# A new interleaving for eight batches: order of the turns, PSUM banks and zero products

## The chip, the cores and the metric

The kernel runs on one core of one Trainium2 chip. The metric is device time in microseconds (us), from three timed runs of the program. PE is the matmul engine and PEld its weight load; DVE, ACT and POOL are the vector, scalar and GpSimd engines; SP issues most of the DMAs. PSUM has eight banks, which only PE writes and only DVE and ACT read.

## What is computed

Four transformer layers over x of 8 batches x 256 rows x 128 features, fp32. Each layer is a gated cross attention to a context of the same shape (16 heads of 8 features) and a gated feed-forward block:

```python
x = x + tanh(g_xattn[l]) * cross_attention_l(layernorm(x), ctx)
x = x + tanh(g_ffn[l])   * ffn_l(layernorm(x))
```

Layer 2's attention is causal; layer 3's keeps only the 51 queries with the highest mean cosine score in each head. The feed-forward blocks are: layer 0 a GELU on the 192 rows with the highest router scores; layer 1 a mixture of 8 gated experts (top 2) and a shared one; layer 2 a mixture of 8 experts of width 512 (top 2, exact GELU) and a shared one; layer 3 one product whose input and weight are rounded to a 6-bit grid.

## The kernel before

Every batch is a stream of the same 286 steps, written out by `stream_steps`: `stats` and `norm` (layer norm), `turn` (transposing the rows), `keys` and `query` (projections), eight `maxima` steps a layer (six in layer 2; a tile of scores on PE, L865, whose row maxima DVE takes, L1389), `max_turn`, eight `attend` steps (scores turned, L888, whose exponential ACT takes, L757) with eight `weigh` steps (probabilities times values, L906), `heads`, `heads_turn`, `project`, and the layer's feed-forward steps: `route0`, `hidden` and `output` (L1046 and L1056 in layer 1, L1077 and L1086 in layer 2), `quantise` and `affine3` in layer 3. Four batches are in flight at once; batch b+4 takes over the buffers of batch b.

One list, `SCHEDULE`, holds the 8 x 286 = 2288 steps in one order, and every engine walks that one list and does its own part of each step. `TURNS_TAKEN` is that order: a string of 2288 digits, each naming the batch whose next step comes. So each engine's instructions stand in the order of the list, and an engine that waits for one step holds all its later ones.

```python
left = [iter([(step, b, l, part) for step, l, part in stream_steps()]) for b in range(BATCHES)]
return [next(left[int(b)]) for line in TURNS_TAKEN.split() for b in line]
```

`BANKS_TAKEN` holds 1857 digits, one for each product that takes a PSUM bank, in the order of the list. Ahead of a product PE waits (`wait_bank`) until the bank's last holder has been read by DVE or ACT. `SCRATCH` names steps ahead of which PE makes a number of products of zeros into the bank that it takes next (L838, 512 columns of bf16): they compute nothing that is used.

PE's products come in four tile forms, by the rows and columns of the array that they use: 128x128 (projections, transposes, feed-forward, zero products), 64x128 (`maxima`, `attend` and the causal masks: two row tiles side by side), 128x32 (`weigh`: four column tiles; `max_turn` and small transposes) and a few with 9 or 16 rows (32x128: `chosen`, `out_bias`). An fp32 product is two passes with a weight load each; a `hidden` step is two pairs of products, into two banks, one after the other.

After a `query` product ACT writes its bf16 high part and the fp32 copy, POOL splits the rest into two more parts (L600, L603, L605), and SP moves the parts with six DMAs (L508) to the rows that the scores read; the first `maxima` of the layer waits for all six.

Of the kernel before, what the change touches and what calls it, by code (L numbers as in the profile page):

```python
# [128 lines left out]


TURNS_TAKEN = """
0002012001311331020003100000202003000101213111001100110011001101200210202020120120023101212121122322
1311102110031333100310120012022101010200300023121022212333232321301012211212131121323313231203031023
3012002320333302023302232220323212300130210303001021010210310101030013033033013301300201333101121210
1212131232212102020000100102121023222102232232212233021211212033320232203210011123020110111010200100
2301322211122011101212121212221122303013303103310321221303030322033232230221332330311202101331103013
0103332200221002012023213310121302102310121222011330221201203032112020210130013311002231322001320100
2012000001001031001313211000110002101010011110211200203011120101112220320103002001111211212123001231
1120220100112001032122101211211221112123302023020012120332002223202003222120300200231111122022120312
0220220012330100031020002001330033010000013013103300002213223230311231103112311332303102231121131123  # L140
1130132112122111111310333101323133101233302233013022002320303000003021303311230130033121124131344411
3111311343142333132232221321555534242353344354443424434322443442342233252223455232234542554544554455
4254544525223453334343455424333545544254242453535535345324434554455354342424552433433452353355323345
3323353322335423325353265366535533635345645644453544344345363466534634434666446466444666663454346453
4334563644366333664366356635336646446564566464565345666356367747546744565656554664674446746546664654
4445757567567557757775747574777547444665455775557676776475774676455775755576554545777655555756575576
7775546555466655445766657464544667667676467776767767456476646564455665446674665666546674665447666666
6566666576766556445747557676744574775547545545574446675756576776747676476475644445477766554547544447
5446664745454575547656775475744475766465774745657767747667454444777766577777566747546577466665547477
4656545766555457544655564474475454455465457577465467774575567667557646755554755674574474576457576766  # L150
6666474665447656747456774644676476756665777776656577557466666664547774644557544765554647567557656764
6774465467557477776777776777777547775545667766765775774645666776764767767457444466764576774455554454
4665477676556566656654656565665564666464665777777567656756676657757776746766547556645776777776657477
4577577767767675775776574777677657475765474564757775647646777647546477767777745757654677
"""


# [9 lines left out]
def signals(step, b, l, part):  # L167
# [44 lines left out]


BANKS_TAKEN = """
1023546012345671002345671023456701253406712503456703124056341203567401236740123406123456701234560123
4501623457620456712405673051246730145261302630245763017634560731425607312674031240673451267034501267
5674520167324501367242501450671245067123045670126745016372450167321452367145671230674501267450124567
0412375604231045623014567230156732017562301474562301627435016235704165234701634572016573240615732641
0567312475612345673401273512640736124012735640123456710237456702340256734256340756120734056741207456
0712560713256071325647132564135264103526401725640175642017536427016534207165430271564302756143027561  # L220
4307265143072561430725614037256147032561470325614730256340172534670125234670123546012345760123456707
1234567013245067132450673124531674531456731456731045367145326745236745672304516702345672304567023407
5614714723470235603417520634175206531725306217503621753061725361072365014762301542367015236740123670
1436701253456701253467015634750167345201762357016572340156723420143560123456017234572013472506134721
5064725106472310645725632304567234567230145671230145674523601734562134721567234015670156347012345671
2045671204536712456312734056712043567012347506123470152347051234017256340172456720145672013452367045
6712031456270134562301425346012576340124576012745601327645013624570126730451236750123067152301675023
4162357014623567401234607120734607123047651247613204762103642701634270162734126734612734126753412567
3041256340125634250172345701234567102375601237560162013756123467512364751326475312653470132650471265
0471265042376145072361045723160457216035472160354726103456712034561234705671203465127034126572301243  # L230
5340712503476123450762304576230764502376145023761452307614507231654072350164523016452301654230165423
0165402316540312653401734560341756340563401756345017634017643107346521076345210745210745712045126045
360124501623456012637450312674503167450324516032745160324
"""

SCRATCH = {
    ("turn", 1, 0, 0): 11, ("keys", 3, 0, 0): 1, ("maxima", 0, 0, 7): 1, ("maxima", 1, 0, 0): 7,
    ("max_turn", 0, 0, 0): 6, ("attend", 0, 0, 0): 1, ("turn", 1, 4, 0): 1, ("turn", 0, 1, 0): 4,  # L240
    ("heads", 2, 0, 0): 1, ("heads", 3, 0, 0): 1, ("heads_turn", 3, 0, 0): 2, ("heads", 0, 1, 0): 1,
    ("heads_turn", 0, 1, 0): 3, ("attend", 1, 1, 0): 4, ("attend", 2, 1, 0): 8, ("heads_turn", 5, 0, 0): 3,
    ("turn", 4, 1, 0): 1, ("turn", 5, 4, 0): 3, ("maxima", 4, 1, 0): 6, ("maxima", 4, 1, 1): 1,
    ("turn", 5, 1, 0): 6, ("maxima", 6, 0, 3): 1, ("heads", 5, 3, 0): 2, ("maxima", 7, 3, 5): 4,
    ("heads_turn", 5, 3, 0): 5, ("heads_turn", 6, 3, 0): 1, ("heads_turn", 7, 3, 0): 5, ("turn", 4, 7, 0): 31}
VALUES_SCRATCH = 7


# [1352 lines left out]
```

How the kernel before makes its waits and increments, by code:

```python
        @block.sync  # L519
# [13 lines left out]
                sp.dma_start(dst, src).then_inc(values_loaded, 16)  # L533
            for s in range(1, SLOTS):
                load_x(s, s)
                load_ctx(s, s)
            w = Walk()
            for w.i, (step, b, l, part) in enumerate(SCHEDULE):
                s = b % SLOTS
                if step == "load_x" and b + SLOTS < BATCHES:
                    sp.wait_ge(sems["xb_ready"], w.at_step("xb_ready", 1, "max_parts", b, 0, 0))
                    load_x(b + SLOTS, s)
                if step == "load_ctx" and b + SLOTS < BATCHES:
                    sp.wait_ge(sems["a_full"], w.at_step("a_full", 1, "keys", b, LAYERS - 1, 0))
                    load_ctx(b + SLOTS, s)
                if step == "load_weight3" and b == 0:
                    sp.wait_ge(sems["a_full"], w.at_step("a_full", 1, "key_mean", b, SPARSE, 0))
                    sp.dma_start(w3_sb, w3).then_inc(w3_loaded, 16)
                if step in ("keys", "query"):
                    name, terms, st, parts = (("k", K_TERMS, k_st[s], k_parts[s]) if step == "keys"
                                              else ("q", Q_TERMS, q_st[s], q_parts[s]))
                    if b < SLOTS and l == 0:
                        sp.wait_ge(*CLEARED[s])
                    if step == "keys" or b >= SPLIT_STREAMS or l > 0:
                        sp.wait_ge(sems[f"hi_ready{s}"], w.at(f"hi_ready{s}", 1))
                        move_parts(sp, terms, 0, st, parts, sems[f"{name}_moved{s}"])
```

## Time and profile before

| | |
|---|---|
| median of 3 runs | 955.25 us (954.61 to 955.75) |
| profiled execution, first to last instruction | 952.3 us |
| the profiled execution's own time | the page gives its span alone; the median lies 2.95 us over it |
| PE busy | 890.7 us |
| DVE busy | 711.9 us |
| ACT busy | 639.7 us |
| POOL busy | 497.8 us |

A piece in the chain of waits or the timeline is a start, a length and what ran. Matmuls are pipelined, so a piece of the timeline ends later than the next one can start; start to start is what a piece costs. In the rows by stretch PEclk is TensorE's granted clock as a share of full speed.

### The profile page before, as it was taken

To read this page: it belongs to the slowest core of one execution; us is meant where nothing else is said; L and a number is where in the kernel's file an instruction comes from. 1 tells how busy PE (TensorE), PEld (TensorE's weight loads), DVE (VectorE), ACT (ScalarE), POOL (GpSimd) and SP (SyncE) were. 2 spreads that over 40 slices of the span, in tenths; PEclk is the share of its full clock that TensorE was granted. 3 is DMA by queue.
4 is the path that set the end of the run, shared out by engine and by line. 5 is a ranking of instruction groups with operands and counts; after the bars stand their busy time and mean duration, and the time that the engine had idled before them with its cause. 6 is when DMAs were issued, how large, how long until landed. Compare 5 with 4: busy or idle time off the path is not lost.

```text
span 952.3 us, 22705 instructions
## 1 busy us (share of the span) xinstructions
PE 890.7 (94%) x8025; PEld 609.1 (64%) x8025; DVE 711.9 (75%) x2175; ACT 639.7 (67%) x1460; POOL 497.8 (52%) x627
## 2 busy tenths in 40 slices
PE   7898889998999999899987999999999999999976
PEld 3344446864799987468643366746588987878533
DVE  6997988868553268986998999887745346666897
ACT  2785766676784635788776677777797448687851
POOL 5446554776872135655356365657772525533172
PEclk9998999999999999999999999999999999999999
DMA  5433341321010010001102121111110010000000
GB/s 149 118 96 83 77 111 30 90 64 37 16 35 23 2 46 7 21 25 51 47 21 68 26 60 34 36 36 36 26 47 2 15 38 1 20 19 18 20 3 24
DMA packets 67520, 39.95 MB, mean 42 GB/s; under 512 B 8263, under 2 KB 65376, under 8 KB 67408
## 3 DMA queue, kind: packets, MB, share of 16 engines
q1 hardware_dynamic: 62608, 30.44, 12.5%
q0 software_dynamic: 2208, 6.78, 2.6%
q8 instruction: 67, 1.10, 0.5%
q10 hardware_dynamic: 2592, 1.26, 0.5%
q14 instruction: 45, 0.37, 0.1%
HBM read 11.12 MB, written 1.05 MB: 13 GB/s over the span
## 4 chain that ended last, share of the span: by engine, by line
PE 63%; DVE 17%; POOL 6%; issue 6%; ACT 5%; DMA 1%; SPq 1%; DVEq 0%; POOLq 0%; ACTq 0%
PE banks L1086 12%; PE banks L1077 12%; PE banks L906 7%; DVE mx L1389 7%; PE banks L1046 6%; PE banks L888 4%; PE banks L865 4%; PE banks L1056 3%; PE banks L851 3%; ACT probs L757 3%; POOL h L617 3%; PE banks L1015 2%; PE banks L844 2%; POOL rn L664 2%; PE banks L955 1%
## 5 line engine op out<-in xcount | busy, mean ns | idle before, releaser
L1389 DVE TENSOR_REDUCE mx<-banks 128x4 f32<-128x1024 f32 (+1 forms) x240 | 283.9, 1216 | 25.0 <-PE banks L865 18.0
L757 ACT ACTIVATE probs<-banks 128x512 f32<-128x512 f32 (+1 forms) x512 | 258.8, 582 | 57.1 <-PE banks L888 53.9
L810 ACT ACTIVATE probs<-banks,b_sb 128x256 f32<-128x256 f32 x288 | 117.9, 474 | 72.9 <-PE banks L1077 71.5
L906 PE MATMUL banks<-probs,v_aug 128*9 128x256 f32 (+1 forms) x2048 | 147.7, 370 | 7.4 <-ACT probs L757 6.2
L1086 PE MATMUL banks<-w_sb,probs 128*128 128x128 f32 x1152 | 140.6, 277 | 0.2 <-ACT probs L757 0.2
L1086 PEld LDWEIGHTS banks<-w_sb,probs 128*128 128x128 f32 x1152 | 134.9, 192 | 5.7 <-issue 2.5
L1077 PE MATMUL banks<-hT,w_sb 128*128 128x256 f32 x576 | 137.4, 382 | 0.1
L610 POOL TENSOR_TENSOR rstd<-veps,mhalf 128x2 f32<-128x2 f32 x64 | 46.3, 724 | 165.3 <-DVE veps L1336 164.7
L664 POOL TENSOR_TENSOR rn<-ss,mhalf 128x32 f32<-128x32 f32 x16 | 88.0, 5501 | 53.2 <-DVE ss L1184 53.1
L1077 PEld LDWEIGHTS banks<-hT,w_sb 128*128 128x128 f32 x576 | 104.4, 190 | 14.8 <-DVE xs L1260 0.8
L1260 DVE SCALAR_TENSOR_TENSOR xs<-banks,comb,xs 128x128 f32<-128x128 f32 x144 | 43.7, 344 | 83.2 <-PE banks L1086 83.0
L888 PE MATMUL banks<-q_st,k_st 64*128 64x256 bf16 (+1 forms) x1024 | 93.9, 269 | 8.9 <-issue 5.7
L865 PE MATMUL banks<-k_st,q_st 64*128 64x256 bf16 (+1 forms) x1024 | 89.0, 265 | 10.4 <-DVE mx L1389 5.1
L617 POOL TENSOR_SCALAR h<-xs,mv,rstd 128x128 f32<-128x128 f32 x112 | 90.9, 818 | 5.9
L888 PEld LDWEIGHTS banks<-q_st,k_st 64*128 64x128 bf16 x1024 | 35.3, 94 | 73.2 <-issue 30.5
L642 POOL TENSOR_TENSOR xs<-xs,raw 128x256 f32<-128x256 f32 x72 | 52.9, 735 | 53.3 <-ACT raw L798 50.8
L1046 PE MATMUL banks<-hT,fc_sb 128*128 128x256 f32 x320 | 77.0, 384 | 0.0
L688 ACT ACTIVATE hT<-banks 128x256 f32<-128x256 f32 x96 | 36.9, 389 | 59.4 <-PE banks L844 59.0
L906 PEld LDWEIGHTS banks<-probs,v_aug 128*9 128x9 f32 x2048 | 34.4, 88 | 62.1 <-ACT probs L757 25.8
L865 PEld LDWEIGHTS banks<-k_st,q_st 64*128 64x128 bf16 x1024 | 37.7, 94 | 56.7 <-issue 18.6
L648 POOL TENSOR_SCALAR_AFFINE_SELECT probs<-probs 128x512 f32<-128x512 f32 x64 | 40.6, 644 | 54.1 <-ACT probs L757 54.0
L1046 PEld LDWEIGHTS banks<-hT,fc_sb 128*128 128x128 f32 x320 | 57.8, 190 | 8.2 <-issue 0.6
(198 smaller groups left out, 1484.0 us busy)
## 6 DMA issues: line engine op xcount, KB each, us to landing
k_st<-k_parts SPq DMA_DIRECT2D x192, 64.0 KB, 2.1
q_st<-q_parts SPq DMA_DIRECT2D x186, 64.0 KB, 2.1
w_sb<-in_w POOLq DMA_DIRECT2D x16, 256.0 KB, 3.7
fc_sb<-in_fc POOLq DMA_DIRECT2D x6, 256.0 KB, 4.3
x_in<-in_x SPq DMA_DIRECT2D x8, 128.0 KB, 4.1
cT<-in_ctxT SPq DMA_DIRECT2D x8, 128.0 KB, 3.1
out_x<-xs SPq DMA_DIRECT2D x8, 128.0 KB, 1.8
q_st<-mT SPq DMA_DIRECT2D x32, 16.0 KB
```

Source lines behind the costliest of these rows:

```text
L617: ins = nc.gpsimd.tensor_scalar(h[s][:, r, :], (x_in if l == 0 else xs)[s][:, r, :], mv[s][:, r, 0:1], rstd[s][:, r:r + 1], ALU.subtract, ...
L642: nc.gpsimd.tensor_tensor(xs[s][:, :, :].rearrange("p t d -> p (t d)"), xs[s][:, :, :].rearrange("p t d -> p (t d)"), raw[s][:, n % OUT_RI ...
L664: nc.gpsimd.tensor_tensor(rn[s][:, :], ss[s][:, :], mhalf[:, :], ALU.pow)\
L757: nc.scalar.activation(probs[s][:, part % UNIT_RING, 2 * a:2 * a + 2, 0:n], b_bank(w, a + 1)[:, 0:2 * n].rearrange("p (j q) -> p j q", j=2 ...
L810: ins = nc.scalar.activation(hid[s][:, part % UNIT_RING, c, :], b_bank(w, half + 1)[:, j * ROWS:(j + 1) * ROWS], ACT.Gelu, bias=b1_sb[:, p ...
L865: ins = nc.tensor.matmul(a_bank(w, a + 1)[:, i * keys:(i + 1) * keys], head_rows(q_st, s, a, hp0 + i, r * P, P), head_rows(k_st, s, a, hp0 ...
L888: ins = nc.tensor.matmul(b_bank(w, a + 1)[:, j * n:(j + 1) * n], head_rows(k_st, s, a, 2 * g + j, t * P, P), head_rows(q_st, s, a, 2 * g + ...
L906: ins = nc.tensor.matmul(c_bank(b, l, u // 4)[VW * i:VW * i + VR, g % 2, q0:ROWS], v_aug[s][:, t, 4 * g + i, :], probs[s][:, u % UNIT_RING ...
L1046: ins = nc.tensor.matmul(a_bank(w, k + 1)[:, a * ROWS:(a + 1) * ROWS], fc1_sb[:, 2 * part + k, a, :], hT[s][:, :], start=True, stop=True)
L1077: ins = nc.tensor.matmul(b_bank(w, half + 1)[:, j * ROWS:(j + 1) * ROWS], w1_sb[:, part, 2 * half + j, :], hT[s][:, :], start=True, stop=True)
L1086: ins = nc.tensor.matmul(a_bank(w, 1)[:, r * D:(r + 1) * D], hid[s][:, part % UNIT_RING, c, r * P:(r + 1) * P], w2_sb[:, part, c, :], star ...
L1389: nc.vector.tensor_reduce(mx[s][:, r, :, hp0:hp0 + n], banks[:, first:first + 2, :].rearrange("p a (n k) -> p a n k", n=n), AX.X, ALU.max) ...
```

## The change

Three tables get new contents, and no instruction of the steps themselves changes: the order (`TURNS_TAKEN`), the banks (`BANKS_TAKEN`), and the places and numbers of the zero products (`SCRATCH`; 28 places with 121 products become 25 with 125). The 2288 steps and 1857 banks stay as many. The new order was searched with a count of PE's changes of tile form among its costs. The two long tables are cut here to their first lines; the third is whole.

```diff
 TURNS_TAKEN = """
-0002012001311331020003100000202003000101213111001100110011001101200210202020120120023101212121122322
+0002102331001320011010220002000000101011033111310110110020012001201200212003020220122103201112122303
...
 BANKS_TAKEN = """
-1023546012345671002345671023456701253406712503456703124056341203567401236740123406123456701234560123
+1022123450612634507123471256341256341721561207534601256734061270346712013452671534126734501267305126
...
 SCRATCH = {
-    ("turn", 1, 0, 0): 11, ("keys", 3, 0, 0): 1, ("maxima", 0, 0, 7): 1, ("maxima", 1, 0, 0): 7,
-    ("max_turn", 0, 0, 0): 6, ("attend", 0, 0, 0): 1, ("turn", 1, 4, 0): 1, ("turn", 0, 1, 0): 4,
-    ("heads", 2, 0, 0): 1, ("heads", 3, 0, 0): 1, ("heads_turn", 3, 0, 0): 2, ("heads", 0, 1, 0): 1,
-    ("heads_turn", 0, 1, 0): 3, ("attend", 1, 1, 0): 4, ("attend", 2, 1, 0): 8, ("heads_turn", 5, 0, 0): 3,
-    ("turn", 4, 1, 0): 1, ("turn", 5, 4, 0): 3, ("maxima", 4, 1, 0): 6, ("maxima", 4, 1, 1): 1,
-    ("turn", 5, 1, 0): 6, ("maxima", 6, 0, 3): 1, ("heads", 5, 3, 0): 2, ("maxima", 7, 3, 5): 4,
-    ("heads_turn", 5, 3, 0): 5, ("heads_turn", 6, 3, 0): 1, ("heads_turn", 7, 3, 0): 5, ("turn", 4, 7, 0): 31}
+    ("maxima", 0, 0, 0): 27, ("query", 2, 0, 0): 4, ("maxima", 1, 0, 0): 2, ("maxima", 1, 0, 1): 2,
+    ("maxima", 1, 0, 2): 1, ("maxima", 1, 0, 3): 5, ("max_turn", 0, 0, 0): 2, ("attend", 0, 0, 0): 1,
+    ("attend", 0, 1, 0): 8, ("attend", 1, 1, 0): 4, ("turn", 3, 1, 0): 2, ("attend", 1, 3, 0): 2,
+    ("turn", 3, 3, 0): 2, ("heads_turn", 4, 0, 0): 2, ("attend", 3, 3, 0): 5, ("maxima", 4, 1, 4): 1,
+    ("maxima", 4, 1, 7): 1, ("attend", 4, 1, 0): 8, ("heads_turn", 3, 3, 0): 3, ("heads_turn", 5, 1, 0): 3,
+    ("maxima", 7, 3, 0): 2, ("maxima", 7, 3, 2): 3, ("maxima", 7, 3, 5): 1, ("heads_turn", 7, 3, 0): 3,
+    ("turn", 4, 7, 0): 31}
```

A key of `SCRATCH` is (step, batch, layer, part).

## Rows read from the trace of the kernel before

**Rows 1.** The page: span, and each engine's busy time, share and instructions.
```profile
span 952.3 us, 22705 instructions
PE 890.7 (94%) x8025; PEld 609.1 (64%) x8025; DVE 711.9 (75%) x2175; ACT 639.7 (67%) x1460; POOL 497.8 (52%) x627
```

**Rows 2.** By stretch: length; busy PE, PEld, DVE, ACT, POOL; PEclk, DMA share, GB/s.
```profile
470.00:600.00 130.00, 117.16 (x1162) 61.75 (x1159) 122.92 (x349) 91.73 (x209) 73.10 (x99) 1.00 0.17 44
...
700.00:900.00 200.00, 199.34 (x1645) 162.66 (x1643) 116.00 (x407) 143.45 (x310) 81.23 (x85) 1.00 0.08 19
...
886.00:952.30 66.30, 52.55 (x489) 26.30 (x487) 56.45 (x229) 31.55 (x67) 28.14 (x32) 0.99 0.06 17
```

**Rows 3.** The chain that ended last, 350 to 358 us: start, length, what.
```profile
350.43 1.79 PE banks L1086 x16
...
352.65 1.73 PE banks L1077 x8
354.37 0.33 PE banks L865 x4
...
354.92 0.22 PE banks L865 x4
...
355.57 1.98 PE banks L1086 x16
```

**Rows 4.** Groups by line and shape: count, busy us, mean ns, idle before and releasers.
```profile
L1389 DVE TENSOR_REDUCE mx<-banks 128x4 f32<-128x1024 f32 x224 | 265.3, 1216 | 21.8 <-PE banks L865 18.0 <-PE banks L873 3.3
L757 ACT ACTIVATE probs<-banks 128x512 f32<-128x512 f32 x448 | 239.3, 608 | 51.4 <-PE banks L888 48.2
...
L906 PE MATMUL banks<-probs,v_aug 128*9 128x256 f32 x1792 | 136.5, 384 | 7.2 <-ACT probs L757 6.2
...
L838 PE MATMUL banks<-zeros 128*128 128x512 bf16 x128 | 34.0, 393 | 5.3 <-DVE mx L1389 3.7 <-ACT resid L724 1.6
...
L844 PE MATMUL banks<-ident,h 128*128 128x128 f32 x128 | 26.2, 289 | 9.3 <-POOL h L617 4.9 <-POOL h L659 2.5 <-DVE h L1345 1.5
```

**Rows 5.** Timelines of PE, ACT, POOL, SP round one query (batch 7, layer 0).
```profile
568.70 0.70 PE L955 MATMUL banks<-hT,wqk 128*128 128x256 f32 x2
...
576.44 0.39 PE L865 MATMUL banks<-k_st,q_st 64*128 64x256 bf16 x4
...
571.58 0.67 POOL L605 TENSOR_TENSOR q_parts<-resid,q_parts 128x256 bf16<-128x256 f32 x1
...
569.93 3.78 SPq L508 DMA_DIRECT2D q_st<-q_parts  x6
```

**Rows 6.** Who waited for whom on PE: us in total, times, longest us.
```profile
PEld banks L906 <- ACT probs L757: 25.8, 72, 1.2
...
PEld banks L865 <- DVE mx L1389: 15.9, 33, 1.0
PEld banks L844 <- DVE resid L1417: 11.8, 16, 1.5
```

**Rows 7.** Short stretches round the low clocks, columns as in rows 2.
```profile
19.10:22.60 3.50, 3.27 (x9) 2.30 (x9) 3.50 (x6) 0.84 (x2) 0.95 (x2) 0.51 0.64 172
...
77.20:80.60 3.40, 1.09 (x8) 0.85 (x8) 1.80 (x6) 0.55 (x2) 2.52 (x5) 1.00 0.86 189
80.60:84.00 3.40, 2.69 (x14) 1.51 (x14) 0.90 (x3) 2.34 (x5) 0.00 (x0) 0.50 0.61 160
84.00:87.40 3.40, 3.40 (x30) 0.83 (x29) 1.62 (x11) 1.09 (x3) 2.01 (x3) 0.50 0.00 0
...
142.00:145.40 3.40, 3.40 (x24) 2.01 (x20) 0.54 (x2) 2.06 (x4) 0.00 (x0) 0.50 0.00 0
```

More of the change, by code:

```diff
@@ L131 @@
 TURNS_TAKEN = """
-0002012001311331020003100000202003000101213111001100110011001101200210202020120120023101212121122322
[L133 to L151, printed above, removed]
@@ L152 @@
-6774465467557477776777776777777547775545667766765775774645666776764767767457444466764576774455554454
-4665477676556566656654656565665564666464665777777567656756676657757776746766547556645776777776657477
-4577577767767675775776574777677657475765474564757775647646777647546477767777745757654677
+0002102331001320011010220002000000101011033111310110110020012001201200212003020220122103201112122303
+2110000303323133110323033301101220120012003212010201231312002211011112133113123112330113122130330222
+1120033300230320230122032210210323200321203100023120010121300013323102330330113301013113320302231010
@@ new lines @@
+1212112012112201233211300123201220103102211022032230122303112200102223300021110210022201201201001120
+0112102111332121222202012121222311233110303322221222100322022303332303010312121033110310030310321230
+0200233121203001201232301013101022101311200232101230333211202023131003031031022022130300211203301123
+1000103000210113001201000100222011220113131101120323000231211301012022230020001200020011211101010030
+1221323122123320311310123111023122221111132310120132310002212122000022202121220022000202330131213112
@@ new lines @@
+1102103021022132321332300101332100100130000320013200033110313001110110101332121100132110301012010321
+2313313021331032302033311131330120302102303020122001231003300323013131013223002414222412423121421221
+2231313412312131313121231123222525433445353442245334442533442434323224433425235253455325442454422545
+4554534543343544345244353433425454544533354552323433543455544544442344425322332233453255322345323333
+4523325323663353365635344644546444534354546565345635654335664543434543564346545646636364346633543463
@@ new lines @@
+3445433364336636466633464566556656656643655645565436663453467677765444454646457654764646646654644454
+5656775477465476757755775447577575477456547675577567447654776675776567776655675757455475565765667766
+7466646564647664755664655565655676465656565757445576654647764666666657774747576667664645754755665545
+5464577466754754755675754675675574567564544455477654745775675774475445777575756467767464754454754566
+4455745756477644544746457547474664454675477776576674774555775775547666757777646564667777666447674474
@@ L155 @@
+4476455655665677746656444564777546667665465747445644756676665564666654777657555657647746657476477475
+7757454655667675676477765766767556675766766656756677567777544467646677767776764574777757555557775674
+7677775555777775657766455667665774767574476757475747646554454456545574475556455465544556455455446575
+7564447545775756656474466456567646767454677676667766476646566576665646476774576674767764757756774755
+4774767475776757774764776547754776756456577667767466465677766774756744777776565456746777
 """
@@ L214 @@
 BANKS_TAKEN = """
-1023546012345671002345671023456701253406712503456703124056341203567401236740123406123456701234560123
[L216 to L233, printed above, removed]
+1022123450612634507123471256341256341721561207534601256734061270346712013452671534126734501267305126
+7045120621456710124503674531426174514356010610761537167617716504157145623456701423556623457623674521
@@ new lines @@
+6014526016721450321064523076067457023167045042546442650120510645764501673456701326452701764520167423
+4501623745203726014263240132564723560124501261261345234564246352461265165243156341207512072514201742
+5601523456206234534601234012763407561561341561340712563470120516345301364573012643567420135426405120
+1152034521735401723541573645635470134203274204723147247317431740563710473470307414710171704130301410
+3043041043034030343010347073014567304634567013676363701301313107364512303540351267435671245614165126
@@ new lines @@
+7412535312675673512456731734562506345062074526012642301430173043407123476237157612353560153674530671
+2304267230467231045067612706410120647026140216026170625372537543267401523017532013475013475201534003
+4512674512067124503160723602367456723014532672323456015635643501267051245610210425640520420513135134
+5165010165021623014672301467230164440612670312346701340125616734156561273405630633673063706456745674
+3126704512346712346721346726234717346247105467065415475047140570123457012364501752306741234516720670
@@ new lines @@
+1672346502346735401345670154672014563740134101562340142305267203427013475632013425343475013501403151
+3407147107532603527025626702675417452012734567230145267364014573670163456701726452301645162346572532
+5236451045607123071704170412310236723015675236014527360137601321362163612074536347051236015320132506
+7234673642051676157570167076010160617235601723707012563470120717071017304217042304237015251023571614
+6237164523610623107071201210272070720702707270107270125634713713456702030562301456723245252340156730
@@ L234 @@
+5634715673415671020362074514071264507321452312374523172451037245603745620560247156204125056120701562
+370175014752301301425402175235725372542334544453543721441
 """
 SCRATCH = {
-    ("turn", 1, 0, 0): 11, ("keys", 3, 0, 0): 1, ("maxima", 0, 0, 7): 1, ("maxima", 1, 0, 0): 7,
-    ("max_turn", 0, 0, 0): 6, ("attend", 0, 0, 0): 1, ("turn", 1, 4, 0): 1, ("turn", 0, 1, 0): 4,
-    ("heads", 2, 0, 0): 1, ("heads", 3, 0, 0): 1, ("heads_turn", 3, 0, 0): 2, ("heads", 0, 1, 0): 1,
-    ("heads_turn", 0, 1, 0): 3, ("attend", 1, 1, 0): 4, ("attend", 2, 1, 0): 8, ("heads_turn", 5, 0, 0): 3,
```

## The prediction

> **What bounds the kernel now.** I read the page first: PE is busy for 94% of the span, DVE for 75% [rows 1]. Then the busy times by stretch, which say where that average holds. From 700 to 900 us PE is busy for 199.3 of 200 us, and DVE for 116; from 470 to 600 us DVE has 122.9 of 130 us and PE 117.2; in the last 66 us DVE has 56.5 and PE 52.6 [rows 2]. So PE sets the time in the feed-forward stretches, and DVE in the middle, where batches 0 to 3 hand over to 4 to 7 and the row maxima crowd (1.216 us each [rows 4]), and at the end. Last the chain of waits, for what one product costs on PE.
>
> A busy PE is not yet a PE at its own pace, so I summed the least start-to-start times. Eight passes of L1077 take 1.73 us and sixteen of L1086 1.79 us where the product before has the same tile form [rows 3]. With the like for every kind, and with each change of form at its price below, all 8025 passes come to 841 us of the 952.3. What lies over that is waits and start, some 104 us, and the largest releasers are the exponentials, the maxima and DVE's other results [rows 6].
>
> **The change, part by part.** No step is added or dropped. I walked both orders through the kernel's own step list and counted.
>
> **Changes of tile form.** A four-pass tile of scores takes 0.22 us behind scores and 0.33 us behind another form, so a change costs 0.11 us. L1086 takes 1.98 us behind one against 1.79 us, 0.19 us, since the second pass's weights aren't hidden either [rows 3]. The old order makes 768 changes, the new one 791, though the search counted them. Into scores 26 more (287 to 313), into two-pass fp32 products 3 more, into `weigh` and small transposes 6 fewer: 26 x 0.11 + 3 x 0.19 - 6 x 0.11 = +2.8 us. The page "TensorE: Matmul & The Clock Gate" of the Trainium skill, section Single matmul latency, puts some 166 ns over the streaming on a product that can't hide its drain; by that an estimate of +3.8 us would stand for these 23 changes. The row decides, and the sum goes on with 2.8.
>
> **Zero products.** 125 in place of 121 at 0.216 us, the time of one pass of 256 fp32 columns (1.73 / 8 [rows 3]), which is also their start to start: +0.9 us. Bounds: nothing, where they fill a wait (their group shows waits for DVE ahead [rows 4]), and +2 us at the low clock. Together PE's own pace grows by 3.7 us.
>
> **Waits for results.** For each step of PE I took PE's own work between it and the step whose result it needs, set it against the least time that the old trace shows for such a hand-over, and counted what is lacking, each wait once (a distance is longer by the waits already counted inside it). For the old order this gives 62 us, stretch by stretch in the places where the trace has its 104. The rest is start-up, low clock and engines that come late, and I take it as equal. For the new order it gives 72 us, in four kinds:
> - A `weigh` behind its exponentials (two of 0.608 us [rows 4]): 9.2 us becomes 4.7.
> - Other hand-overs (`heads` to `heads_turn`, layer norm to `turn`, `max_turn` to `attend`): 27.5 becomes 16.5. `turn` waits on POOL and DVE now [rows 4, 6].
> - The first scores behind their `query`. The last part leaves POOL at 572.25, SP issues six moves for 3.78 us, and the scores start at 576.44, 7.0 us after the query's product ended and 7.4 after its last pass began [rows 5]. The old order leaves PE less than these 7.4 us of its own work in 13 of 32 cases, the new one in 18, often 5.3 to 5.9 us: 10.2 becomes 19.5 us.
> - Banks that PE wants back before they are read. In the old order a quarter of all takings come within 1.83 us of the last holder's product, in the new one within 1.50; short ones rise from 119 to 250. A bank of `turn` or `heads_turn` needs 0.75 us, one of a pair of exponentials 1.5, one of maxima 1.8: 15.4 becomes 31.2 us.
>
> That is -4.5 - 11.0 + 9.3 + 15.8 = +9.6 us. Two stretches I don't take from this count, because DVE binds there. In steps 1050 to 1390 the count says +5.7 us, but DVE's work exceeds PE's by 19.9 us in the old order and 20.2 in the new, so +0.3. From the last layer-2 product on (886 us) DVE's steps sum to 67.8 us by the rows' durations in the old order, 81.0 in the new (eleven maxima and 54 `choose` parts stand behind it, against 8 and 37). The trace makes 56.45 us of the 67.8 [rows 2], so the new ones make 67.4. The stretch had 66.3 us, 9.85 more than DVE's busy time; with the same lag it takes 77.3. PE's own part grows from 46.5 to 53.3 us, which the total holds already, so 11.0 - 6.8 = +4.2 us, against -1.0 in the count. Waits are then 9.6 - 5.4 + 5.2 = +9.4 us. The least times of chains that the old order never presses are too long, by 0.1 to 0.2 us in some 15 places (`heads`, `keys`, `route0`): -2 us. So +7.4.
>
> **The clock.** PEclk is 0.51 in 19.1 to 22.6 us and 0.50 in 80.6 to 87.4 and 142.0 to 145.4, each behind a stretch in which PE did little (1.09 of 3.4 us in 77.2 to 80.6) [rows 7]. The 27 zero products ahead of the first scores (5.8 us) fill the wait before the first fall; but DVE is busy for 3.50 of 3.50 us there, so its going gives nothing. The other two, at most half of 10.2 us, 5 us, may go, or others of that size may come. I take 0.
>
> ACT's table loads, the DMAs and POOL's work stay off the path: ACT and POOL have a quarter of the span free or more [rows 1], and rows 2 show neither at its limit. If that cover went, it would show as longer hand-overs, which are in the bounds.
>
> **Sum.** 3.7 + 7.4 = +11.1 us on a profiled execution of 952.3 us, 963.4; the median lies 2.95 us over that span, so 966.
>
> **The rivals.**
> - *Banks cost nothing (faster).* The mechanism is the choice of banks in the new order: where a bank is taken straight back, the product that takes it waits for a later result anyway, or the reader has come in time. Then the 15.8 us go, and 966.4 - 15.8 = 951 us. For it: the hand-overs to `weigh` and `turn` do get longer distances, and many short takings are of a `query` behind its own `turn`, where PE waits in any case. Against it: the count takes each wait once, and most of the short takings are scores or `hidden` products with no other wait. It decides if PE's waits for banks stay below some 5 us over the old ones.
> - *Pressed banks and late readers (much slower).* With less slack, readers that come late now reach PE. With the fifth percentile of the old trace's hand-over times instead of the least, the count is 75.6 and 97.3 us, +21.7; with 3.7 that is 981 us.
> - *The transfers are hidden.* The waits ahead of a layer's first scores fall into the same time as others, on DVE's side, and the 9.3 us don't show: 957 us, at the edge of no change.
> - *The change doesn't do what it says*: the count of form changes rises rather than falls; that is in the sum.
>
> **How the numbers follow.** The main forecast has 0.45, banks that cost nothing 0.25, hidden transfers 0.14, pressed banks 0.16. A measurement of this kernel tells some 0.2% (1.9 us) from no change. Slower by more is 0.45 + 0.16 + 0.08 of the hidden transfers, 0.69; the other 0.06 of them is no change; faster is 0.25. The likeliest case alone spans 958 to 975 (the clock's 5 us, the zero products' 2 and the correction of 2 either way). Over the cases the range is 948 to 982: below lies the faster rival with a better clock, above the slowest with a worse one.
>
> **What would show it.** In the new profile: the sum of PE, DVE and ACT work as before; L865's idle time ahead of it grown by about 10 us through the DMAs of `q_st`; waits of `hidden` and scores for ACT and DVE readers grown; waits of L906 for L757 and of L844 for its inputs smaller; the stretch behind the last L1086 about 77 us long, with DVE busy for 67; more tiles of L865 and L888 at 0.33 us. I am wrong if PE's waits for banks don't grow, or if the end takes 66 us or less.

## The result and the profile after

The changed kernel takes 969.1 us in the median of four runs (965.41 to 970.47), the kernel before 954.93 (950.34 to 955.75) beside it: ratio 1.0156, 95% interval 1.0134 to 1.0179 (the two medians alone give 1.0148), slower. The forecast was 966 us, in a range of 948 to 982. The profiled execution took 968.79 us with a span of 967.0, 14.7 us more than the span in [rows 1].

The page of the kernel after, its span and busy times:

```profile
span 967.0 us, 22712 instructions
...
PE 898.4 (93%) x8029; PEld 607.3 (63%) x8029; DVE 715.3 (74%) x2175; ACT 639.6 (66%) x1458; POOL 497.9 (51%) x627
```

The work of DVE, ACT and POOL is that of [rows 1] to within 3.4 us, so the 14.7 us are PE's own pace and PE's waits. Four groups by line and shape of the kernel after, columns as in [rows 4]:

```profile
L906 PE MATMUL banks<-probs,v_aug 128*9 128x256 f32 x1792 | 136.3, 382 | 4.9 <-ACT probs L757 3.5 <-ACT raw L764 0.3 <-ACT resid L724 0.3
...
L865 PE MATMUL banks<-k_st,q_st 64*128 64x256 bf16 x896 | 83.6, 276 | 10.8 <-DMA q_st<-q_parts 3.8 <-DVE mx L1389 3.1 <-ACT probs L757 1.9
...
L838 PE MATMUL banks<-zeros 128*128 128x512 bf16 x132 | 37.0, 417 | 17.2 <-DVE mx L1389 5.7 <-DVE resid L1417 3.9 <-DVE junk L1450 2.2
...
L844 PE MATMUL banks<-ident,h 128*128 128x128 f32 x128 | 25.4, 284 | 4.0 <-POOL h L617 2.4 <-POOL h L659 1.0 <-ACT probs L757 0.2
```

The waits that were to shrink did: ahead of `weigh` (L906) 7.2 us became 4.9, ahead of the layer norm's `turn` (L844) 9.3 became 4.0. The zero products (L838) are the surprise: 5.3 us of waiting ahead of them [rows 4] became 17.2. They compute nothing and need no result; all that they can wait for is the bank that they write. PE's waits on others in the kernel after, as in [rows 6], show the same three movements and a wait for the queries' moves that has grown:

```profile
PEld banks L906 <- ACT probs L757: 18.3, 56, 1.0
...
PEld banks L865 <- DVE mx L1389: 13.0, 32, 1.0
PEld banks L865 <- DMA q_st<-q_parts: 10.0, 12, 2.1
...
PEld banks L844 <- DVE resid L1417: 7.7, 11, 1.7
PEld banks L838 <- DVE resid L1417: 5.0, 4, 1.5
```

The wait for the queries' moves in the kernel before:

```profile
PEld banks L865 <- DMA q_st<-q_parts: 1.3, 2, 0.6
```

To put a kind to each wait I took every start-to-start of PE that exceeds, by over 0.05 us, the least that its pair of kinds needs in the old trace, and gave it to the reader or result whose end came last before it. The last column is an experiment, told below.

| waits of PE, us | before | after | change forecast | change measured | new_timed_banks |
|---|---|---|---|---|---|
| banks | 29.7 | 45.2 | +15.8 | +15.5 | 29.7 |
| first scores behind `query` | 0.8 | 5.0 | +9.3 | +4.2 | 8.2 |
| `weigh` behind exponentials | 11.0 | 7.4 | -4.5 | -3.6 | 7.6 |
| other hand-overs | 36.0 | 26.3 | -11.0 | -9.7 | 31.0 |
| not placed | 10.0 | 9.6 | | -0.4 | 11.2 |
| sum | 87.5 | 93.5 | +9.6 | +6.0 | 87.7 |

With what is under 0.05 us each and with the slow clock, all that lies over PE's own pace is 103.8 us before and 111.5 after, +7.7. By the same pairs of kinds the own pace is 841.3 and 847.5 us, +6.2.

The sizes in this table depend on how the products are grouped, the signs don't. A coarser grouping of the same traces (each product by its kind, and by whether the one before it and the one behind it have its tile form) gives an own pace of 836.6 and 840.6 us, +4.0; waits for banks of 30.8 and 55.3 us, and 32.4 in new_timed_banks; and first scores behind their `query` of 1.7, 8.8 and 9.0 us.

Where it lies along the order, in us, from the first product of a step to that of another:

| kernel | to step 300 | 300 to 1050 | 1050 to 1390 | 1390 to end |
|---|---|---|---|---|
| before | 127.0 | 331.6 | 110.7 | 383.0 |
| after | 133.8 | 324.7 | 121.7 | 386.8 |
| new_timed_banks | 128.2 | 322.7 | 119.0 | 384.8 |
| new_then_old | 135.9 | 324.4 | 121.0 | 382.8 |
| old_then_new | 127.9 | 329.1 | 125.0 | 385.0 |
| old_few | 132.0 | 335.0 | 112.6 | 388.6 |
| old_timed_banks | 125.2 | 328.8 | 113.1 | 385.7 |

### The profile page after: what moved, and what is told of

The parts are those of the page before. It is cut to its first block, busy times and chain, and to the rows that moved or that the text cites. A ratio compares the mean times of both kernels' runs of the same rounds, so it can differ in the third digit from the quotient of the medians.

```text
span 967.0 us, 22712 instructions
## 1 busy us (share of the span) xinstructions
PE 898.4 (93%) x8029; PEld 607.3 (63%) x8029; DVE 715.3 (74%) x2175; ACT 639.6 (66%) x1458; POOL 497.9 (51%) x627
## 4 chain that ended last, share of the span: by engine, by line
PE 68%; DVE 15%; ACT 5%; issue 5%; POOL 3%; DMA 2%; SPq 1%; DVEq 0%; POOLq 0%; ACTq 0%
PE banks L1077 13%; PE banks L1086 13%; PE banks L906 7%; PE banks L1046 5%; PE banks L865 5%; PE banks L888 5%; DVE mx L1389 4%; PE banks L851 4%; ACT probs L757 3%; PE banks L1056 3%; PE banks L838 2%; PE banks L1015 2%; PE banks L844 2%; DMA q_st<-q_parts 1%; PE banks L920 1%
## 5 line engine op out<-in xcount | busy, mean ns | idle before, releaser
L1389 DVE TENSOR_REDUCE mx<-banks 128x4 f32<-128x1024 f32 (+1 forms) x240 | 283.9, 1215 | 33.7 <-PE banks L865 26.3
L906 PE MATMUL banks<-probs,v_aug 128*9 128x256 f32 (+1 forms) x2048 | 147.4, 369 | 4.9 <-ACT probs L757 3.5
L1086 PE MATMUL banks<-w_sb,probs 128*128 128x128 f32 x1152 | 141.3, 277 | 0.1
L1077 PE MATMUL banks<-hT,w_sb 128*128 128x256 f32 x576 | 138.9, 386 | 0.1
L1086 PEld LDWEIGHTS banks<-w_sb,probs 128*128 128x128 f32 x1152 | 135.0, 192 | 5.8 <-issue 2.8
L1077 PEld LDWEIGHTS banks<-hT,w_sb 128*128 128x128 f32 x576 | 103.2, 190 | 17.3 <-DVE xs L1260 3.3
L1260 DVE SCALAR_TENSOR_TENSOR xs<-banks,comb,xs 128x128 f32<-128x128 f32 x144 | 43.6, 344 | 79.8 <-PE banks L1086 77.3
L865 PE MATMUL banks<-k_st,q_st 64*128 64x256 bf16 (+1 forms) x1024 | 89.9, 268 | 11.9 <-DMA q_st<-q_parts 4.8
L865 PEld LDWEIGHTS banks<-k_st,q_st 64*128 64x128 bf16 x1024 | 37.4, 95 | 57.7 <-issue 17.6
L906 PEld LDWEIGHTS banks<-probs,v_aug 128*9 128x9 f32 x2048 | 34.7, 88 | 58.4 <-issue 23.5
```

Of the source, the lines that this page charges most:

```text
L865: ins = nc.tensor.matmul(a_bank(w, a + 1)[:, i * keys:(i + 1) * keys], head_rows(q_st, s, a, hp0 + i, r * P, P), head_rows(k_st, s, a, hp0 ...
L906: ins = nc.tensor.matmul(c_bank(b, l, u // 4)[VW * i:VW * i + VR, g % 2, q0:ROWS], v_aug[s][:, t, 4 * g + i, :], probs[s][:, u % UNIT_RING ...
L1077: ins = nc.tensor.matmul(b_bank(w, half + 1)[:, j * ROWS:(j + 1) * ROWS], w1_sb[:, part, 2 * half + j, :], hT[s][:, :], start=True, stop=True)
L1086: ins = nc.tensor.matmul(a_bank(w, 1)[:, r * D:(r + 1) * D], hid[s][:, part % UNIT_RING, c, r * P:(r + 1) * P], w2_sb[:, part, c, :], star ...
L1389: nc.vector.tensor_reduce(mx[s][:, r, :, hp0:hp0 + n], banks[:, first:first + 2, :].rearrange("p a (n k) -> p a n k", n=n), AX.X, ALU.max) ...
```

## The experiments

A median is that of the runs of its group, and each ratio is to the kernel before on the same chip.

**Halves of the change.** Four kernels take a part of the change each. new_other_banks and old_other_banks replace the table of banks in the new and in the old order by one that a plain rule gives (the bank whose reader has been done longest, by the sums of the prediction):

```diff
 BANKS_TAKEN = """
-1022123450612634507123471256341256341721561207534601256734061270346712013452671534126734501267305126
+0123456721034567012345671234560123457601234571023645671023450162340156273457016534675034526701523460
...
```

> The new order and the new zero products, with the 1857 banks given anew: each product takes the bank whose last reader was done longest ago (a pair of neighbours for scores and heads), improved a little by single changes. Theory: banks taken back too early cost the new kernel about 15 us more than the old one; by PE's own distances the counted waits for banks fall from 31.3 to 14.2 us, and all waits, each counted once, from 71.9 to 64.7. So about 7 us faster than the new kernel: 962 us, with fewer stalls on readers of L1389 and L757. Rival (banks cost nothing, the products wait for a later result anyway): 969 us, within 2.

Measured: 971.31 us, ratio 1.0178 (1.0156 to 1.02).

> The old order and old zero products, with banks given by the same rule of the longest done reader. It is the control for the rule. The count for the old order is 15.5 us of waits for banks with its own banks and 21.4 with these, all waits 62.3 and 67.4. Theory (banks count): about 5 us slower than the old kernel, 960 us. Rival (banks cost nothing): 955, within 2.

Measured: 974.24 us, ratio 1.0218 (1.0198 to 1.0237). The same rule costs the old order 20 us and the new one 2, so the first of the two, read alone, would have said that banks don't matter. With its control it says only that the rule is bad: it has no rows of when a reader really ends, and the waits put to banks rise from 29.7 to 50.8 us in the old order. What the control does show is that the table of banks by itself can be worth 2%.

new_old_zeros is the kernel after with the zero products of the kernel before:

```diff
 SCRATCH = {
-    ("maxima", 0, 0, 0): 27, ("query", 2, 0, 0): 4, ("maxima", 1, 0, 0): 2, ("maxima", 1, 0, 1): 2,
...
+    ("turn", 1, 0, 0): 11, ("keys", 3, 0, 0): 1, ("maxima", 0, 0, 7): 1, ("maxima", 1, 0, 0): 7,
...
```

> The new order and banks, with the old kernel's table of zero products (the same steps, 121 products). This tells the table of zero products from the order. PE's own pace falls by 2.5 us (779 changes of form in place of 791, four products fewer); the waits that the new table fills come back: 81.0 us counted in place of 71.9. Theory (the order and its banks carry the loss): 969 to 976 us, since zero products mostly stand in waits. Rival (the zero products and the 20 or so changes of form that they bring carry the loss): 960 us or less.

Measured: 972.72 us, ratio 1.0201 (1.0177 to 1.0225). The loss isn't in where the zero products were put: with the old places it is as large or a little larger.

new_then_old has the new order, banks and zero products to step 1050 and the old ones behind, for the steps that are left (three banks had to be changed at the seam):

```diff
 TURNS_TAKEN = """
...
-2231313412312131313121231123222525433445353442245334442533442434323224433425235253455325442454422545
+2231313412312131313121231123222525433445353442245335434443434434434233252223455232234542554544554455
...
```

> The new order, its banks and zero products up to step 1050, then all that is left in the old order with the old banks and zero products (three banks changed at the seam). In both traces step 1050 begins 458.5 us from the start, so what the new order loses in steps 0 to 300 it has won back by there. Theory: the loss of the new kernel lies behind step 1050, so this one takes the old kernel's time and what the seam costs: 955 to 960 us. Rival (a part in the first 1050 steps hands its loss on to what follows, through batches that stand less far): 965 to 970 us.

Measured: 962.32 us, ratio 1.0093 (1.0069 to 1.0116), between the two. Its row in the table by stretch says more than its time: 1050 to 1390 takes 121.0 us though the old order stands there, and what follows takes the old time.

**Banks by the trace.** new_timed_banks keeps the new order and the new zero products, and chooses each bank by the ends of the readers in the trace of the kernel after; old_timed_banks does so for the old order from its own trace.

```diff
 BANKS_TAKEN = """
-1022123450612634507123471256341256341721561207534601256734061270346712013452671534126734501267305126
+0112125673401234567012304567012345012675341207645301275634051260345621072314675123456712034567012345
...
```

> New order and zero products, but each product takes its bank by the changed kernel's own trace: the one whose reader ended with most to spare (searched over the whole list, pairs kept side by side). In that trace 84 takings start less than 0.12 us behind the reader of their bank, 26.6 us in all; with these banks, at the same times, 24 do, 7.4 us. Theory (the new table of banks carries the loss): the difference of 19 us goes, and the time falls to 950 to 956 us. Rival (behind each wait for a bank PE would have waited for a result anyway, or the engines that read have no time to spare): not under 963 us. Second rival (the stretch from step 1050 to 1390, where DVE sets the pace, doesn't move with the banks, all else does): 958 to 962.

Measured: 956.3 us, 12 runs, ratio 1.0034 (1.0011 to 1.0056). Of the 15 us that the change costs (ratio 1.0156) some 12 go with this one table. The first theory holds, at the upper end of what it gave and far from the rival's 963 us. The second rival's premise holds too, but for little: from step 1050 to 1390 the time moved only from 121.7 to 119.0 us, while the first 300 steps got back 5.6 us (133.8 to 128.2).

> Control: old order and zero products, banks chosen in the same way from the old kernel's trace. There 26 takings start less than 0.12 us behind their reader, 7.4 us, and with these banks 21 would, 5.0 us. Both theories: 950 to 956 us, no difference or a small gain. If the way of choosing is itself at fault, as the rule of the second run was (+20 us on the old order), it shows here, and the run before says nothing against the banks.

Measured: 955.04 us, 12 runs, ratio 1.0013 (0.9997 to 1.0029): no difference. So the old table was already as good as this way of choosing makes one, and the new table wasn't.

The gain isn't the clock's alone, though the clock has a part in it. (The mean granted clock is that of a whole run, as a share of full speed.) The runs of new_timed_banks differ by 9 us, the slowest with the lowest mean granted clock (962.38 us at 0.983, 953.33 at 0.996). At the same clock of 0.996 a run of the kernel after took 965.41 us, so 12 us lie between the two tables there too, run for run.

One number of those two expectations was poor. Of the 1857 takings 80 have a last holder whose reader I hadn't matched; I had set its end 1.5 us behind the product, and most of the 26.6 us came from them. Without them, the takings within 0.3 us of their reader's end are 253 before, 438 after, 171 in new_timed_banks and 228 in old_timed_banks. They tell the same.

One place shows how a bank costs time. PE's timeline of the kernel after:

```profile
102.67 0.39 PE L865 MATMUL banks<-k_st,q_st 64*128 64x256 bf16 x4
105.24 2.45 PE L838 MATMUL banks<-zeros 128*128 128x512 bf16 x8 [2.18 <-DVE junk L1450]
107.62 0.61 PE L888 MATMUL banks<-q_st,k_st 64*128 64x256 bf16 x4
```

And DVE's, with the last reading of the router's bank, then the same steps on PE in new_timed_banks:

```profile
104.70 0.47 DVE L1450 SCALAR_TENSOR_TENSOR junk<-banks,col,before 128x256 f32<-128x256 f32 x1
```

```profile
99.31 0.39 PE L865 MATMUL banks<-k_st,q_st 64*128 64x256 bf16 x4
99.79 1.90 PE L838 MATMUL banks<-zeros 128*128 128x512 bf16 x8
102.26 0.40 PE L888 MATMUL banks<-q_st,k_st 64*128 64x256 bf16 x4 [0.57 <-DVE junk L1450]
```

SP's move of the row maxima, which this `attend` needs, in the kernel after and in new_timed_banks:

```profile
103.23 0.58 SPq L569 DMA_DIRECT2D q_st<-mT  x1
```

```profile
100.28 0.58 SPq L569 DMA_DIRECT2D q_st<-mT  x1
```

Eight zero products stand ahead of an `attend` to fill its wait for that move. (The last row names L1450 in its place; but in new_timed_banks L1450 had ended at 101.66, and the scores start 1.98 us behind the start of the move.) In the kernel after the bank of the zero products is the router's, which DVE reads until 105.17, some 1.94 us behind the start of the move; so they start only when the wait that they should fill is over, and the scores come 4.95 us behind the tile before (102.67 to 107.62). With another bank they run inside the wait, and it is 2.95 us. Over the whole kernel the waiting ahead of L838 falls back from 17.2 us to 5.0, with the same 132 products in the same places (125 of `SCRATCH` and seven that both kernels have at the start). Group of new_timed_banks:

```profile
L838 PE MATMUL banks<-zeros 128*128 128x512 bf16 x132 | 34.6, 395 | 5.0 <-DVE mx L1389 3.4 <-ACT probs L757 1.1 <-ACT resid L724 0.4
```

The first group, the 27 ahead of the first scores, in the kernel after and in new_timed_banks:

```profile
11.55 7.33 PE L838 MATMUL banks<-zeros 128*128 128x512 bf16 x27 [1.41 <-DVE v_aug L1309]
```

```profile
11.13 5.99 PE L838 MATMUL banks<-zeros 128*128 128x512 bf16 x27
```

In the first the products wait for a bank, and the granted clock is 0.50 from 10.9 to 14.3 us. In the second they don't wait, and the clock is 1.00 over the first 514 us. This suggests that a wait for a bank costs clock too; no run sets the clock apart.

old_then_new is the other half, old to step 1050 and new behind:

```diff
 TURNS_TAKEN = """
...
-3111311343142333132232221321555534242353344354443424434322443442342233252223455232234542554544554455
+3111311343142333132232221321555534242353344354443422222423442434323224433425235253455325442454422545
...
```

> The other half: the old order, banks and zero products up to step 1050, then the new order's for the steps that are left. The changed kernel lost 10.9 us from step 1050 to 1390 and 3.8 us behind. With the new order up to 1050 and the old one behind it, the stretch 1050 to 1390 still took 121.0 us, against 110.7 in the old kernel, and what follows took the old time. Theory (what the order up to 1050 leaves over for the stretch of the maxima sets its length): it now takes some 111 us, and the whole 956 to 959 us. Rival (the new arrangement behind 1050 costs by itself): the stretch takes 118 us or more, and the whole 964 to 969 us.

Measured: 970.46 us, ratio 1.017 (1.0142 to 1.0197): the rival's side and past its range, with 125.0 us from 1050 to 1390. As the new order up to 1050 with the old one behind it had also lost there, neither half carries the loss alone: each mixture of the two orders is longer there than the old one, with banks that weren't chosen for it. By the coarser grouping their waits for banks are 45.5 us (new_then_old) and 50.4 (old_then_new) against 30.8 in the kernel before, so the banks are the likelier cause; no run gives these two orders, unchanged, banks by their own traces.

**Fewer changes of form.** new_few takes new_timed_banks and moves 43 steps by one to five places, each where PE's own pace and the counted waits together came out lower; old_few does it with 26 steps of the old order, hyb_few with 40 of new_then_old. The banks are chosen again from the traces. The first moves of old_few:

```diff
 TURNS_TAKEN = """
-0002012001311331020003100000202003000101213111001100110011001101200210202020120120023101212121122322
+0002012001311331020003100000202003000110213111001100110011001101202010202020120120023101212121122322
...
```

> The changed order with 43 steps moved by one to five places so that PE changes its tile form less often: 737 times in place of 791 (into scores 287 in place of 313, into 128x32 tiles 229 in place of 240, into two-pass fp32 products 134 in place of 144); banks chosen as in new_timed_banks, zero products as in the change. Theory (a change of form is paid on PE, 0.11 us into scores and small tiles and 0.19 us into a two-pass product): 26 x 0.11 + 11 x 0.11 + 10 x 0.19 = 6.0 us less than the 956.3 us of new_timed_banks, so 948 to 952. Rival (a change of form mostly stands beside a wait, and steps drawn together press the banks or wait for their results instead): 955 to 959.

Measured: 966.11 us, ratio 1.0136 (1.0121 to 1.0152).

> The same on the order of before: 26 steps moved, 732 changes in place of 768 (into scores 276 in place of 287, small tiles 240 in place of 250, two-pass 132 in place of 141), banks by the old kernel's own trace. Theory: 21 x 0.11 + 9 x 0.19 = 4.0 us less than the 955.0 us of old_timed_banks, so 949 to 953. Rival: 954 to 957.

Measured: 965.26 us, ratio 1.0124 (1.0109 to 1.014).

> New order up to step 1050 and the old one behind it (new_then_old, 962.3 us), 40 steps moved (736 changes in place of 791: 36 fewer into scores and small tiles, 12 fewer two-pass), and banks by the trace of new_then_old, where 56 takings stand less than 0.12 us behind their reader, 16.8 us in all; with the new banks 28 would, 7.1 us. Theory (both the banks and the changes of form are paid): 9.7 us and 36 x 0.11 + 12 x 0.19 = 6.2 us less, so 944 to 950. Rival (the stretch 1050 to 1390 stays at some 121 us, since DVE sets it): 953 to 958.

Measured: 974.59 us, ratio 1.0222 (1.0199 to 1.0245). All three lose some 10 us and more where they were to gain 4 to 16, so even the rivals were too kind. By the pairs of kinds PE's own pace did fall, from 841.3 to 836.4 us in old_few, but what lies over it rose from 104.3 (old_timed_banks) to 124.4. Pressed banks aren't the cause: by the coarser grouping the waits for them are 33.7 us in old_timed_banks and 34.1 in old_few. A part is the clock. Its mean in the two profiled runs is 0.987 and 0.977; with the two levels 1 and 0.5 that is an estimated 25 and 45 us at the lower one, worth at most half of the difference, 10 of the 20 us. The clock falls behind waits, so it makes each of them dearer; what the moves cost without it no run shows. One of the 26 moves is 2.7 us of the rise. `max_turn` of batch 3 was put three places later, beside a `weigh`, and so behind a `query`. PE and SP in old_few:

```profile
76.18 0.70 PE L955 MATMUL banks<-hT,wqk 128*128 128x256 f32 x2 [0.47 <-ACT hT L688]
76.81 0.23 PE L995 MATMUL banks<-mask_b,m_parts 128*32 128x128 bf16 x1
...
78.70 1.09 PE L1015 MATMUL banks<-ident,raw 128*128 128x128 f32 x8 [0.25 <-ACT raw L764]
84.97 0.61 PE L888 MATMUL banks<-q_st,k_st 64*128 64x256 bf16 x4 [5.18 <-DMA q_st<-mT]
```

```profile
77.42 4.50 SPq L508 DMA_DIRECT2D q_st<-q_parts  x6
81.97 0.58 SPq L569 DMA_DIRECT2D q_st<-mT  x1
```

The same places in the kernel before, PE and SP:

```profile
77.50 1.09 PE L1015 MATMUL banks<-ident,raw 128*128 128x128 f32 x8 [0.40 <-ACT raw L764]
81.05 0.61 PE L888 MATMUL banks<-q_st,k_st 64*128 64x256 bf16 x4 [2.46 <-issue]
```

```profile
76.13 0.58 SPq L569 DMA_DIRECT2D q_st<-mT  x1
76.76 3.76 SPq L508 DMA_DIRECT2D q_st<-q_parts  x6
```

The move of the maxima (L569) used to leave SP ahead of the query's six; now it stands behind them. From the `heads` (L1015) of another batch to the `attend` that needs this move, PE takes 6.27 us (78.70 to 84.97) in place of 3.55 (77.50 to 81.05). The clock falls behind that wait in both: it is 0.50 from 80.6 to 87.4 in the kernel before [rows 7], and in old_few for some 10 us from 83.2. The stretch in old_few, columns as in [rows 7]:

```profile
83.00:86.40 3.40, 1.43 (x10) 0.58 (x10) 0.00 (x0) 0.81 (x2) 0.00 (x0) 0.53 0.21 42
86.40:89.80 3.40, 3.14 (x24) 1.31 (x24) 1.45 (x10) 1.54 (x4) 0.59 (x1) 0.50 0.00 0
```

**The price of a change of form.** Since moving steps moves waits too, two kernels add changes without moving any step: a product of zeros with 16 columns between the halves of each of the 72 layer-2 `output` steps of the kernel before, in the form of its neighbours or in that of the scores.

```diff
 for r in range(RT):
+    if r == 1:
+        nc.tensor.matmul(a_bank(w, 1)[:, D:D + 16], zeros[0:P, 0:P], zeros[0:P, 0:16], start=True, stop=True)
     for c in range(HC):
```

form_half has zeros[0:HALF, ...] in both places.

> Control for the price of a change of tile form: the kernel before, with one product of zeros, 16 columns of bf16 in the 128x128 form, between the two halves of each of the 72 layer-2 output steps (8 passes of L1086, the zeros, 8 passes). No step moves, no wait is added, no form changes. It takes the price of a short product among passes of its own form: 72 times 0.03 to 0.15 us, 956 to 965 us.

Measured: 959.68 us, ratio 1.0062 (1.0039 to 1.0085).

> The same 72 products of zeros from 64 rows, in the form of the scores: 144 changes of form, 72 into a one-pass product and 72 back into a two-pass one. Theory (a change is paid as the prediction priced it, wherever it stands): 72 x (0.11 + 0.19) = 21.6 us more than the control, less what waits take up, so 15 to 22 us. In the profile, from the last pass of the first half to the first of the second it lasts 0.30 us longer than in the control. Rival (the 0.11 and 0.19 us belong to the kinds of products that met there, not to the form): under 5 us more than the control.

Measured: 973.2 us, ratio 1.0218 (1.0192 to 1.0243). PE in form_full, then in form_half (L1086 is L1088 here, and the zeros have L1086):

```profile
708.78 1.06 PE L1088 MATMUL banks<-w_sb,probs 128*128 128x128 f32 x8
709.68 0.17 PE L1086 MATMUL banks<-zeros 128*128 128x16 bf16 x1
709.71 1.14 PE L1088 MATMUL banks<-w_sb,probs 128*128 128x128 f32 x8
710.68 0.60 PE L920 MATMUL banks<-cT,wqk 128*128 128x256 f32 x2
```

```profile
707.12 1.05 PE L1088 MATMUL banks<-w_sb,probs 128*128 128x128 f32 x8
708.10 0.18 PE L1086 MATMUL banks<-zeros 64*128 64x16 bf16 x1
708.21 1.16 PE L1088 MATMUL banks<-w_sb,probs 128*128 128x128 f32 x8
709.21 1.04 PE L1015 MATMUL banks<-ident,raw 128*128 128x128 f32 x8
```

The step takes 1.90 us in the first (708.78 to 710.68) and 2.09 in the second. Over all 72, the step from its first pass to its last has a mean of 1.706 us before, 1.814 and 2.012: 0.108 us for the short product and 0.198 for the two changes. 72 x 0.108 = 7.8 us and 72 x 0.198 = 14.3; the times differ by 7.7 and 13.5, short of the theory's 15 to 22 and far from the rival's 5. So a change of form is paid almost whole in the time here, at 0.10 us each way beyond the control (0.096 ahead of the zeros, 0.102 behind them). For the change into the scores' form that is nearly the price of 0.11. For the one back it looks like half of the 0.19, but the control already pays the other half: behind a short product of their own form the eight passes take 0.08 us longer. Where L1086 stands right behind scores both halves show. PE in the kernel before:

```profile
355.19 0.38 PE L865 MATMUL banks<-k_st,q_st 64*128 64x256 bf16 x4
355.50 2.05 PE L1086 MATMUL banks<-w_sb,probs 128*128 128x128 f32 x16
357.39 1.89 PE L1077 MATMUL banks<-hT,w_sb 128*128 128x256 f32 x8
```

From start to start the scores take 0.31 us in place of 0.22 and L1086 takes 1.89 in place of 1.79 [rows 3], 0.19 us together. So form_half doesn't lower that price.

## Why the prediction held, step by step

**Forecast and theory.** The likeliest case was right in sign and, to 3 us, in size, and for the reason it gave first: banks wanted back before they are read. It gave +15.8 us for them, and new_timed_banks takes some 12 us of the change's 15 away with the banks alone. The table of waits has +15.5, the coarser grouping +24.5, so the agreement to 0.3 us is luck. With those banks the new order has as many waits as the old one in sum (87.7 and 87.5 us).

**Own pace, +3.7 us.** The changes of form were priced about right: from pass to pass they are 26 x 0.096 + 3 x 0.19 - 6 x 0.10 = 2.5 us where the sum had 2.8. (The 6 fewer are 10 fewer into 128x32 tiles and 4 more into one-pass products of 128x128.) By the rule on a product's latency that the prediction cites (Trainium skill, "TensorE: Matmul & The Clock Gate", Single matmul latency) it would have been 3.8; form_half, with 0.10 us a change, doesn't bear that out. The sum over pairs of kinds gives +6.2 us for the own pace in all, and the coarser grouping +4.0. So the term was right or too small by 2.5 us; no run measures it apart.

**Hand-overs.** `weigh` -3.6 us against -4.5, the others -9.7 against -11.0: right. The first scores behind their `query` rose by 4.2 us by the table and by 7.1 by the coarser grouping, not by 9.3; the wait that the profile gives grew from 1.3 to 10.0 us. So the transfers aren't hidden, but the term was too large. The 7.4 us that it needs were read from scores that follow a `weigh` at once (576.44), and so had no wait to show. After, the same hand-over (batch 2, layer 2) is shorter:

```profile
217.34 0.67 PE L955 MATMUL banks<-hT,wqk 128*128 128x256 f32 x2
...
224.01 0.40 PE L865 MATMUL banks<-k_st,q_st 64*128 64x128 bf16 x8
```

That is 6.67 us from start to start, against 7.74 [rows 5].

**The step that failed: where DVE binds.** The prediction left the count aside in steps 1050 to 1390 (+5.7 us) for a difference of work, DVE's over PE's, and took +0.3. The stretch grew by 11.0 us, and 7.5 of it lie over PE's own pace (7 by the coarser grouping): the count that was set aside was nearer. Before and after, 300 to 1050 and 1050 to 1390:

```profile
127.00:458.60 331.60, 320.16 (x2816) 244.39 (x2819) 229.98 (x719) 224.59 (x530) 182.81 (x222) 0.99 0.16 40
458.60:569.30 110.70, 98.70 (x998) 50.88 (x997) 103.69 (x318) 76.10 (x165) 58.54 (x77) 1.00 0.17 43
```

```profile
133.80:458.50 324.70, 316.96 (x2802) 238.37 (x2801) 225.28 (x721) 231.13 (x533) 180.72 (x217) 1.00 0.15 39
458.50:580.20 121.70, 104.87 (x1006) 56.70 (x1004) 110.14 (x321) 77.78 (x166) 59.41 (x82) 0.97 0.17 43
```

DVE (fourth number) has 6.5 us more to do in the second stretch, 4.7 us less in the first, where it had a third of its time free; and in the second it is also idle for 11.6 us against 7.0. The prediction saw DVE's work against PE's, not that work had moved in from a stretch with room. What it lost there it got back by luck, for 300 to 1050 gained 6.9 us: the total of the waits came out at +7.7 (forecast +7.4) through misplacements that cancel.

How much of those 11.0 us is the order, how much the clock, stays open: two slow stretches lie there, behind maxima that wait for banks. After, columns as in [rows 7]:

```profile
517.00:519.50 2.50, 1.11 (x10) 0.35 (x9) 2.50 (x3) 0.38 (x1) 2.40 (x4) 0.99 0.32 79
519.50:522.90 3.40, 3.06 (x16) 1.12 (x15) 3.40 (x4) 0.84 (x2) 1.20 (x2) 0.50 0.16 39
522.90:526.30 3.40, 3.40 (x19) 1.86 (x18) 3.40 (x5) 0.84 (x2) 1.53 (x3) 0.50 0.40 101
```

new_timed_banks still takes 119.0 us there, with DVE busy for 109.4. But DVE's work doesn't set the length alone: new_then_old and old_then_new, with 106.8 and 107.3 us of it, take 121.0 and 125.0.

**The end.** The stretch behind the last L1086 was to take 77.3 us with DVE busy for 67.4. After, columns as in [rows 2]:

```profile
891.40:967.00 75.60, 60.97 (x590) 28.88 (x588) 65.74 (x274) 41.55 (x87) 29.58 (x34) 0.95 0.06 15
```

75.6 and 65.7 us: right, with the same lag over DVE's work (9.9 us).

**The clock** was taken as nothing gained or lost. The first fall came earlier (10.9 us), ahead of the 27 zero products, which waited for their bank; the ones round 80 and 142 us lie round 86 and 106, the first half as long; one of 6.8 us came at 519 us, and a longer one at the end (946 to 953). From the mean clocks, 0.992 and 0.987, an estimated 15 us became 25 at the lower level, worth at most 5 us: within the 5 us given, but all of them.

**The signs to look for.** Seen: L865 waiting for the DMAs of `q_st`, as 10.0 us in 12 times; L906 and L844 waiting less; the end; and a little of the `hidden` products' wait for DVE's reader (L1077 for L1260: 0.8 to 3.3 us). Not seen: waits of the scores for the maxima fell (15.9 [rows 6] to 13.0 us), because zero products now stand first in line and take the wait, as L838's row shows. A sum by line would have called the banks harmless; only with L838's row does the sum by cause come right.

**The rivals.** That banks cost nothing is refuted by new_timed_banks, that transfers are hidden by the 10.0 us above; pressed banks with late readers (981 us) lay too high, as the hand-overs got shorter, not later. That the number of changes rises though it was searched was so (768 to 791), and costs some 2.5 us.

No version was faster than the kernel before. The best of the new order, 956.3 us, is 0.34% over the kernel before.

## What to carry to other kernels

Where banks or buffers are handed out by a table, make the table from the ends of the readers in a trace, and check a rule on a kernel whose table is known to be good before its verdict on another counts. A product that only fills a wait must not take a bank that is read until the wait is over. A cost in an order search, such as changes of tile form, is worth its price only while no step is moved past something else in any queue: one `max_turn` put behind a `query` saved two changes, at 0.10 us each, and cost 2.7 us through SP.

## What the runs showed of the hardware that was not expected

A product of 16 columns among two-pass products of its own form costs 0.108 us, though only 0.03 us lie between its start and the next one's (709.68 to 709.71). The other 0.08 us show in the eight passes behind it. A change of tile form costs 0.10 us in either direction; behind scores, L1086 takes another 0.10 us from its first pass to its second (0.213 in place of 0.112 in the kernel before). SP's six moves of a query, all of one size, take from 3.74 to 4.90 us within one trace, that of the kernel before.
